# Work for the next attention layer, placed beside the last expert tiles of a two-layer decoder: sums in halves and later, first differences on another engine, row maxima behind the tiles

## The chip, the cores and the metric

One Trainium2 chip, one core of it. The metric is the device time of one execution in microseconds (us), the median of three runs. The core has a tensor engine (PE), a vector engine (VectorE, DVE in the rows), a scalar engine (ScalarE, ACT), GpSimd (POOL) and SyncE (SP), which here only issues DMAs. Each engine runs its own instructions in their written order, and the engines wait for each other through semaphores.

## The reference

Two decoder layers on x of shape (4, 512, 128) in float32: four batches of 512 tokens. Each layer is attention, cross-attention to a context of 77 keys, and a feed-forward part, each on a layer norm of x and added to x. The feed-forward part of layer 0 is a mixture of eight experts with the best two per token. What lies around the change:

```python
x = x + _L0_attn_ref(_layernorm(x, axis=-1), ...)        # causal, 16 heads of 8
x = x + _L0_xattn_ref(_layernorm(x, axis=-1), ctx_1024, ctx_1024, ...)
x = x + _L0_ffn_ref(_layernorm(x, axis=-1), ...)         # 8 experts, top 2 of them per token
x = x + _L1_attn_ref(_layernorm(x, axis=-1), ...)        # not causal, 16 heads of 8
x = x + _L1_xattn_ref(_layernorm(x, axis=-1), ctx_1024, ctx_1024, mask_1xSxS2_ff0, ...)
x = x + _L1_ffn_ref(_layernorm(x, axis=-1), ...)
```

## The kernel before

The core runs a first stream (attention and cross-attention of layer 0, 32 units of four heads and one batch each), then the experts (`moe_pe`, `moe_act`, `moe_dve`, `moe_pool`, `moe_sp`), then a second stream (attention of layer 1, here A1, 16 units, and the last layers).

**The expert tiles.** The tokens were scattered into rows sorted by expert. `BUSY_TILES` is 39: tiles t = 0 to 38 of 128 rows each. Every engine has a loop over t, in which its parts of neighbouring tiles stand in a fixed order:

- SP: the row number is read into a register (L1966), a wait for `y_at` of tile t-2 (L1969), the load of tile t into `x_in` (L1970), then `ahead_sp(e, t)`.
- PE: first half of the hidden layer of t+1 (L1897), turn of tile t+2 (L1888, a transpose, which waits for that tile's load), second half of the hidden layer of t+1, output of t (L1905), then `ahead_pe(e, t)`.
- ScalarE: SiLU of t (L1945), half of the weights of t+2 (L1935), `ahead_act(e, t)`.
- VectorE: `turned` of t+2 (L1753, L1754), `product` of t+1 (L1762), half of the weights of t+3 (L1767), `output` of t (L1774), `ahead_dve(e, t)`.
- GpSimd: the scatter of the finished tile t to HBM (L1874), which waits for VectorE's output of t, then `ahead_pool(e, t)`.

So in one round t the engines are not at the same tile: SP's load of t+4 follows VectorE's `turned(t+2)` of round t.

**The `ahead` functions** put work of the second stream between the rounds, each piece at a round t that is written out by hand. For batches 0 and 1 of x: from tile 22 on (`HALF_TILES` is 23) the outputs for these two batches are complete. `fetch_sp` brings them back from HBM (L1978, two DMAs of 512 KB). `combine_dve` adds the two weighted expert outputs to x (L1816, eight instructions of 128x128, four for each of the two experts). Then come the moments (L469 to L475), their root on GpSimd (L496), the norm (L490), its transpose on PE (L547), the copy (L561), and the q, k and v products (L864, L882).

**The three parts.** q and k are split into three bf16 parts that add up to the float32 value. `stage1_act` writes the first part (L1331) and a float32 copy `qf` (L1333, named `cos_sin` in the rows). GpSimd makes the first difference `rest = qf - part1` (L1344), ScalarE rounds it to the second part (L1337), and GpSimd makes the third (L1347). When the third is there, `stack_dma` writes the parts to HBM (L954, three DMAs of 384, 256 and 128 KB for q or for k), and `load_sp` loads them back in the layout of the heads (L663, L669, into `stk`). After that the row maxima of the scores can be made: `max_pe` (L598) and `max_dve` (L614), 16 of each for one unit of A1, then `neg_of` on GpSimd (L629, L631) and its transpose `turn_pe` (L636), with which the unit's scores can begin.

**PSUM banks.** `take_bank` hands out banks in turn; beside the tiles only two are free (`bank_scores[:, 3]` and `bank_pv`), behind them four.

Of the kernel before, what the change touches and what calls it, by code (L numbers as in the profile page):

```python
# [245 lines left out]

def qf_read_by(a, b, z):

    if a is X0 or b == 0:
        return split_number(a, b, 0 if a is A1 else z)  # L250
    return split_number(a, b - 1, z) + 1
# [11 lines left out]
def build(nc, d, out):  # L263
# [4 lines left out]
    with es:  # L268
# [650 lines left out]
        def split_pool(e, a, b, z, step):  # L919
# [10 lines left out]
            elif step == 2:  # L930
                e.wait_ge(s["rest"], n + 1)
# [395 lines left out]
        def stage1_act(e, b, z):  # L1327
# [4 lines left out]
            e.wait_ge(s["rest"], qf_read_by(A1, b, z))  # L1332
            e.activation(qf[:, z], bank_of(key), ACT.Identity, bias=bias).then_inc(is_emptied(key), 1)  # L1333

        def part2_act(e, b, z):
            e.wait_ge(s["rest"], split_number(A1, b, z) + 1)
            e.copy(parts[:, z, 1], rest[:, z]).then_inc(s["part2"], 1)  # L1337

        def split1_pool(e, b, z, step):
            n = split_number(A1, b, z)  # L1340
            if step == 0:
                e.wait_ge(s["part1"], n + 1)
                e.wait_ge(*emptied(("qk"[z], A1.ln, b)))
                e.tensor_tensor(rest[:, z], qf[:, z], parts[:, z, 0], ALU.subtract).then_inc(s["rest"], 1)  # L1344
            else:
                e.wait_ge(s["part2"], n + 1)
                e.tensor_tensor(parts[:, z, 2], rest[:, z], parts[:, z, 1], ALU.subtract).then_inc(s["part3"], 1)  # L1347
# [6 lines left out]
        def ahead_pe(e, t):  # L1354
            if t in (27, 33):
                norm_pe(e, A1.ln, t // 33)
            elif t == 28:
# [3 lines left out]
            elif t in (29, 36):  # L1361
                for part in range(2):
                    stage_v_pe(e, A1, t // 36, part)
            elif t in (34, 35):
                for part in range(2):
                    stage_q_pe(e, A1, 1, t - 34, part)
            elif t in (37, 38):
                for k in range(FIRST * (t - 37), FIRST * (t - 36)):
                    max_pe(e, A1.first, k)

        def ahead_act(e, t):
            if t in (29, 35):
                norm_act(e, A1.ln, t // 35)
            elif t in (30, 31):
                stage1_act(e, 0, t - 30)
            elif t == 32:
                part2_act(e, 0, 0)
                stage_v_act(e, A1, 0)
            elif t == 33:
                part2_act(e, 0, 1)  # L1380
            elif t in (36, 37):
                stage1_act(e, 1, t - 36)
            elif t == 38:
                part2_act(e, 1, 0)
                stage_v_act(e, A1, 1)
                part2_act(e, 1, 1)

        def ahead_dve(e, t):
            if t == 24:
                e.wait_ge(m["gates"], 1)  # L1390
            if t in (24, 28):
                combine_dve(e, 2, t // 28)
            elif t in (25, 30):
                moments_dve(e, A1.ln, t // 30)
            elif t in (26, 32):
                normalise(e, A1.ln, t // 32)
            elif t in (37, 38):
                for k in range(FIRST * (t - 37), FIRST * (t - 36)):
                    max_dve(e, A1.first, k)

        def ahead_pool(e, t):
            if t == 25:
                norm_pool(e, A1.ln, 0)
            elif t in (29, 35):
                split1_pool(e, t // 35, 0, 0)
            elif t in (30, 36):
                split1_pool(e, t // 36, 1, 0)
                if t == 30:
                    norm_pool(e, A1.ln, 1)
            elif t in (31, 37):  # L1410
# [1121 lines left out]
```

## Time and profile before

| | us |
|---|---|
| median of three runs | 761.88 (761.59, 761.88, 763.45) |
| the profiled execution | 766.63 |
| its span | 764.9 |
| PE busy | 645.7 (84%) |
| VectorE busy | 563.5 (74%) |
| ScalarE busy | 431.0 (56%) |
| GpSimd busy | 305.0 (40%) |
| tile 0 to 38, VectorE's outputs start | 346.2 to 474.2 |

The profiled execution took 4.75 us more than the median, and 1.7 us of it lie outside its span. The rows are of that one execution. "Full" clock of PE is 2.4 GHz (1.00 in the rows), half is 1.2 GHz (0.50). L12 is line 12 of the kernel as printed above. The L1774 instruction is run once per tile, 39 times; the 25th (tile 24) starts at 413.20, the 33rd (tile 32) at 450.56, the 35th (tile 34) at 457.13 and the last (tile 38) at 474.18.

### The profile page before, as it was taken

The numbers are of one execution on the slowest core, as the hardware profiler recorded it, in microseconds if no ns is written. First come the engines' busy times: TensorE is split into PE (matmuls) and PEld (weight loads), VectorE is DVE, ScalarE is ACT, GpSimd is POOL, SyncE is SP. The second block draws the span as 40 slices with busy tenths as digits, with TensorE's granted clock in tenths as the row PEclk, the third lists the DMA queues.
The fourth block names the chain that finished last, engine by engine and source line by source line (L and its number), as shares of the span: only waits on it lengthen the run. The fifth ranks groups of instructions, "written<-read, shape, count | busy, mean of one in ns | idle before, by whom it ended". The sixth has DMA issues, their size and how long they took to land.

```text
span 764.9 us, 16027 instructions
## 1 busy us (share of the span) xinstructions
PE 645.7 (84%) x5015; PEld 354.0 (46%) x5020; DVE 563.5 (74%) x1664; ACT 431.0 (56%) x825; POOL 305.0 (40%) x536
## 2 busy tenths in 40 slices
PE   5679998999978887239997987899999989897987
PEld 2344454444434444239997885133323323234543
DVE  6977688687737786747776686899998898924564
ACT  1415565566665654025664454478887777884644
POOL 6653454545551335723332354275251341421310
PEclk9867998999988999559999898599999999999998
DMA  7744564453233311211113126210413110000000
GB/s 229 253 162 146 174 197 142 127 179 99 75 87 85 110 45 67 78 36 47 50 47 92 35 72 213 98 57 30 139 51 116 30 55 30 2 1 1 15 15 28
DMA packets 72802, 67.17 MB, mean 88 GB/s; under 512 B 14560, under 2 KB 67232, under 8 KB 72720
## 3 DMA queue, kind: packets, MB, share of 16 engines
q1 hardware_dynamic: 69920, 61.21, 25.9%
q0 software_dynamic: 2272, 4.69, 1.9%
q8 instruction: 42, 0.69, 0.4%
q14 instruction: 40, 0.33, 0.1%
q10 hardware_dynamic: 528, 0.26, 0.1%
HBM read 37.74 MB, written 28.00 MB: 86 GB/s over the span
## 4 chain that ended last, share of the span: by engine, by line
PE 54%; DVE 23%; issue 9%; POOL 5%; ACT 4%; DMA 3%; SPq 1%; DVEq 0%; ACTq 0%; POOLq 0%
DVE mx L614 13%; PE bank_pv L761 11%; PE bank_turn L598 7%; PE bank_scores L2165 5%; PE bank_scores L713 4%; PE bank_scores L1897 4%; PE bank_turn L1897 4%; PE bank_scores L1905 4%; PE bank_turn L780 3%; POOL routed_tokens L1858 3%; DVE stats L469 2%; PE bank_turn L602 1%; DVE xn L490 1%; PE bank_turn L822 1%; ACT probs L734 1%
## 5 line engine op out<-in xcount | busy, mean ns | idle before, releaser
L614 DVE TENSOR_REDUCE mx<-bank_turn 128x1 f32<-128x512 f32 (+4 forms) x438 | 251.3, 612 | 45.7 <-PE bank_turn L602 29.6
L713 PE MATMUL bank_scores<-stk 64*128 64x512 bf16 (+3 forms) x576 | 172.6, 363 | 4.2 <-ACT probs L734 3.0
L598 PE MATMUL bank_turn<-stk 64*128 64x77 bf16 (+4 forms) x694 | 151.3, 305 | 27.8 <-DVE mx L614 18.7
L738 ACT ACTIVATE probs<-bank_scores 128x1024 f32<-128x1024 f32 (+4 forms) x160 | 116.8, 768 | 94.8 <-PE bank_scores L713 93.7
L734 ACT ACTIVATE probs<-bank_scores 128x512 f32<-128x512 f32 x256 | 139.1, 605 | 33.9 <-PE bank_scores L713 33.1
L761 PE MATMUL bank_pv<-probs,vsl 128*32 128x512 f32 (+3 forms) x1152 | 139.3, 556 | 2.9 <-POOL probs L746 1.8
L598 PEld LDWEIGHTS bank_turn<-stk 64*128 64x128 bf16 x694 | 52.0, 98 | 123.9 <-DVE mx L614 58.0
L746 POOL TENSOR_SCALAR_AFFINE_SELECT probs<-probs 128x256 f32<-128x256 f32 x128 | 51.6, 407 | 75.2 <-ACT probs L738 73.5
L1874 POOL DMA_INDIRECT expert_outputs<-probs,y_at x39 | 37.9, 972 | 95.4 <-DVE y_at L1754 61.3
L713 PEld LDWEIGHTS bank_scores<-stk 64*128 64x128 bf16 x576 | 45.8, 94 | 27.5 <-ACT probs L734 15.4
L496 POOL TENSOR_TENSOR rstd<-var,mhalf 128x4 f32<-128x4 f32 x24 | 24.7, 1028 | 78.3 <-DVE var L475 77.9
L614 DVE TENSOR_REDUCE mx<-bank_scores 128x1 f32<-128x512 f32 x73 | 49.7, 680 | 8.0 <-PE bank_scores L598 7.7
L602 PE MATMUL bank_turn<-masked_key,later_key 64*128 64x64 bf16 x512 | 51.3, 201 | 0.0
L602 PEld LDWEIGHTS bank_turn<-masked_key,later_key 64*128 64x128 bf16 x512 | 46.0, 103 | 11.3 <-issue 3.1
L2165 PE MATMUL bank_scores<-f_w1c,w 128*128 128x512 f32 x96 | 46.1, 618 | 0.4 <-ACT w L556 0.4
L1897 PE MATMUL bank_scores<-probs,w_now 128*128 128x128 f32 x304 | 41.9, 287 | 5.4 <-DVE probs L1753 5.4
L1905 PE MATMUL bank_scores<-w,oT 128*128 x312 | 42.9, 282 | 1.6 <-DVE probs L1774 1.6
L1897 PE MATMUL bank_turn<-probs,w_now 128*128 128x128 f32 x320 | 42.9, 284 | 0.0
L1897 PEld LDWEIGHTS bank_scores<-probs,w_now 128*128 128x128 f32 x304 | 39.5, 203 | 5.8 <-DVE probs L1753 5.7
L1897 PEld LDWEIGHTS bank_turn<-probs,w_now 128*128 128x128 f32 x320 | 40.9, 201 | 0.1
L1905 PEld LDWEIGHTS bank_scores<-w,oT 128*128 128x128 f32 x312 | 39.1, 197 | 2.3 <-issue 2.3
L761 PEld LDWEIGHTS bank_pv<-probs,vsl 128*32 128x32 f32 x1152 | 23.2, 109 | 33.3 <-issue 25.7
(310 smaller groups left out, 1062.6 us busy)
## 6 DMA issues: line engine op xcount, KB each, us to landing
stk<-stack_A SPq DMA_DIRECT2D x64, 256.0 KB, 3.1
w<-in_M_w SPq DMA_DIRECT2D x12, 512.0 KB, 4.4
stack_A<-parts SPq DMA_DIRECT2D x12, 384.0 KB, 2.7
stack_A<-fill SPq DMA_DIRECT2D x8, 512.0 KB, 5.0
stk<-stack_X SPq DMA_DIRECT2D x16, 256.0 KB, 2.7
stack_A<-parts SPq DMA_DIRECT2D x12, 256.0 KB, 3.1
probs<-routed_tokens SPq DMA_DIRECT2D x39, 65.0 KB, 1.9
stack_A<-parts SPq DMA_DIRECT2D x12, 128.0 KB, 2.9
```

The source lines that it names most:

```text
L598: mm = e.matmul(o, stk[r, slot, 0, pp, qt * P:(qt + 1) * P], stk[r, slot, 1, pp, 0:keys], start=True, stop=not a.causal)
L602: mm = e.matmul(o[:, qt * P + HR * k:qt * P + HR * (k + 1)], later_keys(j, k), masked_keys(j), start=False, stop=k == 1)
L614: e.tensor_reduce(o.rearrange("p h q -> p q h"), bank_of((g, m))[:, 0:k * keys].rearrange("p (q h k) -> p q h k", q=len(tiles), h=len(hs)) ...
L713: mm = e.matmul(score_bank(g, kt, i)[:, 0:S - q0], stk[r, slot, 1, pp, kt * P:(kt + 1) * P], stk[r, slot, 0, pp, q0:S], start=True, stop=True)
L734: e.activation(probs[:, probs_of(g, kt), j + 2 * pp], score_bank(g, kt, i), ACT.Exp, scale=1 / math.sqrt(HD)).then_inc(s["probs"], 1)
L738: e.activation(probs[0:a.kp, probs_of(g, kt), j:HG:2, 0:n], bank_scores[0:a.kp, 2 * j:2 * j + 2, 0:n], ACT.Exp, scale=1 / math.sqrt(HD)).t ...
L746: e.affine_select(out=o, in_=o, compare_op=ALU.is_ge, fill=0.0, base=0, pattern=[[0, 2], [1, P]], channel_multiplier=-1).then_inc(s["maske ...
L761: mm = e.matmul(bank_pv[VW * h:VW * (h + 1), q0:S], vsl[:, slot, kt, h, :], probs[:, probs_of(g, kt), h, 0:S - q0], start=(kt == 0), stop= ...
L1874: e.indirect_dma_start(scr_y, bass.IndirectOffsetOnAxis(ap=y_at[:, t:t + 1], axis=0), y_sb[:, t % 2], None).then_inc(m["stored"][t % 2], 16)
L1897: mm = e.matmul(hid[t % 2][z][:, c * P:(c + 1) * P], w_now[:, t % 2, o:o + P], x_inT[:, t % 2], start=True, stop=True)
L1905: mm = e.matmul(y_bank[:, 0:D], act[:, t % 2, c * P:(c + 1) * P], w2[:, bass.ds(ex[t], 1), c, :].rearrange("p o n -> p (o n)"), start=(c = ...
L2165: e.matmul(bank, f_xT[:, b, j * P + tap:j * P + tap + P], f_w1c[:, tap], start=(tap == 0), stop=False)
```

## The change

Only the work beside tiles 24 to 38 and what follows it directly is touched. `combine_dve` does four instructions at a time: batch 0 at rounds 25 and 26 instead of all eight at 24, batch 1 at 29 and 30 instead of 28. Moments move from 25 and 30 to 27 and 31, norms from 26 and 32 to 28 and 32, PE's transposes from 27 and 33 to 29 and 34, q and k of batch 0 from 28 to 31, and so on. The float32 copy `qf` and GpSimd's first difference are gone: VectorE computes it from the PSUM bank in one instruction (`rest1_dve`, bias added, first part subtracted). No maxima are made beside the tiles; all 16 of unit 32 follow them. Of batch 1, v's copy, the second parts and the third parts are made behind the tiles, its stacks after the shift of the first unit.

```diff
+        def rest1_dve(e, b, z):
+            key, n, bias = ("qk"[z], A1.ln, b), split_number(A1, b, z), wts["A1"]["bk" if z else "bq"][:]
+            e.wait_ge(s["part1"], n + 1)
+            e.wait_ge(s["part3"], n - 1 if b else 3 * NB + 1)
+            e.scalar_tensor_tensor(rest[:, z], bank_of(key), bias, parts[:, z, 0], ALU.add, ALU.subtract)\
+                .then_inc(is_emptied(key), 1)
...
-        def split1_pool(e, b, z, step):
...
+        def part3_1_pool(e, b, z):
+            e.wait_ge(s["part2"], split_number(A1, b, z) + 1)
+            e.tensor_tensor(parts[:, z, 2], rest[:, z], parts[:, z, 1], ALU.subtract).then_inc(s["part3"], 1)
...
         def ahead_dve(e, t):
-            if t == 24:
+            if t == 25:
                 e.wait_ge(m["gates"], 1)
-            if t in (24, 28):
-                combine_dve(e, 2, t // 28)
+            if t in (25, 26):
+                combine_dve(e, 0, t - 25)
+            elif t in (29, 30):
+                combine_dve(e, 1, t - 29)
...
+            elif t in (32, 33):
+                rest1_dve(e, 0, t - 32)
+                if t == 32:
+                    normalise(e, A1.ln, 1)
+            elif t in (37, 38):
+                rest1_dve(e, 1, t - 37)
...
         def ahead_pool(e, t):
...
+                part3_1_pool(e, 0, t - 34)
...
         def ahead_sp(e, t):
             if t == 27:
                 fetch_sp(e, 0)
-            elif t == 37:
-                stack_dma(e, A1, 0, 0)
+            elif t in (36, 37):
+                stack_dma(e, A1, 0, t - 36)
             elif t == BUSY_TILES - 1:
-                stack_dma(e, A1, 0, 1)
                 for g in range(A1.first, A1.first + UNITS):
                     load_sp(e, g)
+                fetch_sp(e, 1)
+                shift_sp(e, A1.first)
                 for z in range(2):
                     stack_dma(e, A1, 1, z)
-                shift_sp(e, A1.first)
-                fetch_sp(e, 1)
...
         def second_stream_pe(e):
...
-            for k in range(2 * FIRST, len(A1.items)):
-                max_pe(e, A1.first, k)
+            all_maxima_pe(e, A1.first)
...
         def second_stream_act(e):
+            stage_v_act(e, A1, 1)
+            for z in range(2):
+                part2_act(e, 1, z)
```

What this does to three queues is seen in the order of their instructions (line numbers are of the kernel whose order it is). On SP, before, from the load of tile 36 over that of tile 37 (both into `probs`), q's stack of batch 0 and the load of tile 38 to k's stack:

```order
L1966 TENSOR_LOAD tile_row
L1966 ISA x2
L1970 ISA [waits M0_y_at,M0_xT]
L1970 DMA probs<-routed_tokens 128x130
L954 DMA stack_A<-parts 128x3x512 [waits att_part3]
L954 DMA stack_A<-parts 128x2x512
L954 DMA stack_A<-parts 128x512
L1966 TENSOR_LOAD tile_row
L1966 ISA x2
L1970 ISA [waits M0_y_at,M0_xT]
L1970 DMA probs<-routed_tokens 128x130
L954 DMA stack_A<-parts 128x1536 [waits att_part3]
```

On SP now, from the load of tile 36 over q's stack, the load of tile 37 and k's stack to the row number of tile 38:

```order
L1966 DMA probs<-routed_tokens 128x130
L959 DMA stack_A<-parts 128x3x512 [waits att_part3]
L959 DMA stack_A<-parts 128x2x512
L959 DMA stack_A<-parts 128x512
L1962 TENSOR_LOAD tile_row
L1962 ISA x2
L1966 ISA [waits M0_y_at,M0_xT]
L1966 DMA probs<-routed_tokens 128x130
L959 DMA stack_A<-parts 128x1536 [waits att_part3]
L959 DMA stack_A<-parts 128x1024
L959 DMA stack_A<-parts 128x512
L1962 TENSOR_LOAD tile_row
```

The stacks moved up: before, q's stack stood behind the load of tile 37 and k's behind that of tile 38, the last; now they stand behind the loads of 36 and 37. On GpSimd, before, behind the scatter of tile 29 (scatters are `expert_outputs`, the first differences L1344 and the third parts L1347 of batch 0 stand between them):

```order
L1344 TENSOR_TENSOR rest<-cos_sin,parts 128x512 [waits emptied4,att_part1]
L1874 DMA expert_outputs<-probs,y_at 4116x128 [waits M0_y_out,M0_y_at]
L1344 TENSOR_TENSOR rest<-cos_sin,parts 128x512 [waits emptied3,att_part1]
L496 TENSOR_TENSOR rstd<-var,mhalf 128x4 [waits s_var]
L1874 DMA expert_outputs<-probs,y_at 4116x128 [waits M0_y_out,M0_y_at]
L1347 TENSOR_TENSOR parts<-rest,parts 128x512 [waits att_part2]
L1874 DMA expert_outputs<-probs,y_at 4116x128 [waits M0_y_out,M0_y_at]
L1347 TENSOR_TENSOR parts<-rest,parts 128x512 [waits att_part2]
```

On GpSimd now, the same kinds of instruction, from the scatters of tiles 32 to 34 to that of tile 36:

```order
L1870 DMA expert_outputs<-probs,y_at 4116x128 [waits M0_y_out,M0_y_at] x3
L1351 TENSOR_TENSOR parts<-rest,parts 128x512 [waits att_part2]
L1870 DMA expert_outputs<-probs,y_at 4116x128 [waits M0_y_out,M0_y_at]
L1351 TENSOR_TENSOR parts<-rest,parts 128x512 [waits att_part2]
L1870 DMA expert_outputs<-probs,y_at 4116x128 [waits M0_y_out,M0_y_at]
```

Batch 0's third parts followed the scatters of tiles 31 and 32; now they follow those of 34 and 35, and the first differences are no longer here. On VectorE, before, from the output of tile 24 (L1774) over batch 0's sums (L1816) to the turned tile 27 (L1753):

```order
L1774 TENSOR_TENSOR probs<-bank_scores,b_rows 128x128
L1816 SCALAR_TENSOR_TENSOR x_sb<-got,gate,x_sb 128x128 [waits M0_got0,M0_gates]
L1816 SCALAR_TENSOR_TENSOR x_sb<-got,gate,x_sb 128x128 x3
L1816 SCALAR_TENSOR_TENSOR x_sb<-got,gate,x_sb 128x128 [waits M0_weighed] x4
L1753 COPY probs<-bank_turn 128x128 [waits M0_weighed,M0_xT]
```

On VectorE now, one tile later, from the output of tile 25 (L1770) over the first half of the sums (L1811) to the turned tile 28 (L1749):

```order
L1770 TENSOR_TENSOR probs<-bank_scores,b_rows 128x128
L1811 SCALAR_TENSOR_TENSOR x_sb<-got,gate,x_sb 128x128 [waits M0_got0,M0_gates]
L1811 SCALAR_TENSOR_TENSOR x_sb<-got,gate,x_sb 128x128 x3
L1749 COPY probs<-bank_turn 128x128 [waits M0_xT]
L1750 SCALAR_TENSOR_TENSOR y_at<-probs,tile_f 128x1
```

Four of the eight sums are left there; the other four follow the output of tile 26.

## Rows read from the trace of the kernel before

**Rows 1.** Busy time by stretch: engines, granted clock, DMA share, GB/s.
```profile
345.00:390.00 45.00, 45.00 (x406) 45.00 (x405) 33.56 (x130) 26.69 (x82) 14.91 (x16) 1.00 0.18 48
...
414.00:419.00 5.00, 1.35 (x13) 1.16 (x11) 2.19 (x8) 1.25 (x4) 0.96 (x1) 0.95 0.48 166
419.00:422.00 3.00, 2.62 (x12) 2.62 (x13) 2.92 (x16) 0.39 (x2) 0.22 (x1) 0.50 0.09 22
...
474.00:484.00 10.00, 5.89 (x16) 1.14 (x16) 7.88 (x14) 0.00 (x0) 3.08 (x5) 0.50 0.29 106
```
**Rows 2.** Timeline of VectorE, tiles 23 to 26: start, duration, line, idle before.
```profile
410.40 0.28 DVE L1774 TENSOR_TENSOR probs<-bank_scores,b_rows 128x128 f32<-128x128 f32 x1
...
411.82 1.13 DVE L1762 SCALAR_TENSOR_TENSOR oT<-bank_scores,b_cols,probs 128x128 f32<-128x128 f32 x4 [0.58 <-ACT probs L1945]
...
413.20 0.28 DVE L1774 TENSOR_TENSOR probs<-bank_scores,b_rows 128x128 f32<-128x128 f32 x1
416.70 2.19 DVE L1816 SCALAR_TENSOR_TENSOR x_sb<-got,gate,x_sb 128x128 f32<-128x128 f32 x8 [3.23 <-DMA got<-expert_outputs]
...
422.27 0.17 DVE L475 TENSOR_SCALAR var<-mv 128x4 f32<-128x4 f32 x1
```
**Rows 3.** The chain that ended last, in order of time: start, duration.
```profile
405.20 0.89 PE bank_scores L1897 x8
...
410.92 5.68 DMA got<-expert_outputs
...
419.38 2.08 PE bank_scores L1897 x8
421.67 1.71 PE bank_scores L1897 x8
```
**Rows 4.** SP's issues, two stretches: start, duration of issuing.
```profile
410.92 0.94 SPq L1978 DMA_DIRECT2D got<-expert_outputs  x2
412.67 0.36 SPq L1970 DMA_DIRECT2D probs<-routed_tokens  x1
...
454.39 1.69 SPq L954 DMA_DIRECT2D stack_A<-parts  x3
457.84 0.36 SPq L1970 DMA_DIRECT2D probs<-routed_tokens  x1
```
**Rows 5.** DMA issues with time to landing: the load at 412.67.
```profile
probs<-routed_tokens SPq DMA_DIRECT2D x1, 65.0 KB, 5.7
```
**Rows 6.** The same view: the load at 457.84.
```profile
probs<-routed_tokens SPq DMA_DIRECT2D x1, 65.0 KB, 1.9
```
**Rows 7.** VectorE's timeline: moments beside GpSimd, outputs of tiles 32, 34.
```profile
443.73 1.73 DVE L475 TENSOR_SCALAR var<-mv 128x4 f32<-128x4 f32 x1
...
450.56 0.28 DVE L1774 TENSOR_TENSOR probs<-bank_scores,b_rows 128x128 f32<-128x128 f32 x1
...
457.13 0.29 DVE L1774 TENSOR_TENSOR probs<-bank_scores,b_rows 128x128 f32<-128x128 f32 x1
```
**Rows 8.** GpSimd's timeline: first difference, scatter of tile 32, third part.
```profile
444.26 1.16 POOL L1344 TENSOR_TENSOR rest<-cos_sin,parts 128x512 f32<-128x512 f32 x1
...
451.59 0.98 POOL L1874 DMA_INDIRECT expert_outputs<-probs,y_at  x1 [1.25 <-DVE probs L1774]
452.61 1.16 POOL L1347 TENSOR_TENSOR parts<-rest,parts 128x512 bf16<-128x512 f32 x1
```
**Rows 9.** One line of VectorE: min/median/max ns.
```profile
L1293 DVE SCALAR_TENSOR_TENSOR probs<-bank_scores,A_bq,cos_sin x4: 735/738/750, 13.8 to 41.0; 128x512 f32<-128x512 f32 x4
```
**Rows 10.** PE's timeline: turn of unit 32.
```profile
483.54 0.29 PE L636 MATMUL bank_turn<-identb,neg 128*32 128x128 bf16 x1 [2.40 <-POOL neg L631]
```
**Rows 11.** VectorE's timeline: output of tile 38, maxima of unit 32.
```profile
474.18 0.29 DVE L1774 TENSOR_TENSOR probs<-bank_scores,b_rows 128x128 f32<-128x128 f32 x1 [0.97 <-PE bank_scores L1905]
...
478.00 1.88 DVE L614 TENSOR_REDUCE mx<-bank_turn 128x1 f32<-128x512 f32 x3
...
482.19 0.68 DVE L614 TENSOR_REDUCE mx<-bank_scores 128x1 f32<-128x512 f32 x1
```

More of the change, by code:

```diff
@@ L1360, in ahead_pe @@
                         stage_q_pe(e, A1, 0, z, part)
-            elif t in (29, 36):
+            elif t in (33, 38):
                 for part in range(2):
-                    stage_v_pe(e, A1, t // 36, part)
-            elif t in (34, 35):
[L1365 to L1368, printed above, removed]
-                    max_pe(e, A1.first, k)
[L1371 to L1386, printed above, removed]
@@ L1388, in ahead_dve @@
-        def ahead_dve(e, t):
-            if t == 24:
-                e.wait_ge(m["gates"], 1)
-            if t in (24, 28):
-                combine_dve(e, 2, t // 28)
[L1393 to L1410, printed above, removed]
-                split1_pool(e, t // 37, 0, 1)
-            elif t in (32, 38):
-                split1_pool(e, t // 38, 1, 1)
-            elif t == 34:
+                    stage_v_pe(e, A1, t // 38, part)
+            elif t in (36, 37):
+                for part in range(2):
+                    stage_q_pe(e, A1, 1, t - 36, part)
@@ new lines, in ahead_act, with ahead_dve @@
+        def ahead_act(e, t):
+            if t in (31, 36):
+                norm_act(e, A1.ln, t // 36)
+            elif t in (32, 33):
+                stage1_act(e, 0, t - 32)
+            elif t == 34:
+                part2_act(e, 0, 0)
+            elif t == 35:
+                part2_act(e, 0, 1)
+                stage_v_act(e, A1, 0)
+            elif t in (37, 38):
+                stage1_act(e, 1, t - 37)
+        def ahead_dve(e, t):
+            if t == 25:
+                e.wait_ge(m["gates"], 1)
+            if t in (25, 26):
+                combine_dve(e, 0, t - 25)
+            elif t in (29, 30):
+                combine_dve(e, 1, t - 29)
+            elif t in (27, 31):
+                moments_dve(e, A1.ln, t // 31)
+            elif t == 28:
+                normalise(e, A1.ln, 0)
+            elif t in (32, 33):
+                rest1_dve(e, 0, t - 32)
+                if t == 32:
+                    normalise(e, A1.ln, 1)
+            elif t in (37, 38):
+                rest1_dve(e, 1, t - 37)
@@ L1415, in ahead_pool @@
+        def ahead_pool(e, t):
+            if t in (27, 31):
+                norm_pool(e, A1.ln, t // 31)
+            elif t in (34, 35):
+                part3_1_pool(e, 0, t - 34)
+            elif t == 36:
                 values_pool(e, A1.first)
@@ L1559, in second_stream_dve @@
         def second_stream_dve(e):
-            for k in range(2 * FIRST, len(A1.items)):
-                max_dve(e, A1.first, k)
+            all_maxima_dve(e, A1.first)
             turn_dve(e, A1.first)
@@ L1577, in second_stream_pool @@
             neg_of(e, A1.first)
+            for z in range(2):
+                part3_1_pool(e, 1, z)
             bias_pool(e, A1, 0)
```

50 lines of the change are left out of this document (21 added, 29 removed).

## The prediction

> **What bounds the kernel now.** I read the busy times by stretch first, then the chain that ended last, then the timelines of VectorE, PE, GpSimd and SP between tiles 24 and 38, and the times from issue to landing.
>
> In the tiles, PE is the bound: busy 45.00 of 45 us at full clock [rows 1]. A tile takes 2.79 us, from one output of VectorE to the next (410.40 to 413.20), and VectorE waits 0.58 us for ScalarE in it [rows 2]. PE's three groups of eight take 0.89 each at full clock and 1.71 at half, the turn 0.11 and 0.21 (2.79 less three times 0.89, and twice that) [rows 3].
>
> At tile 24 that ends. VectorE, with the output of tile 24 issued at 413.20, waits 3.23 us for batch 0's expert outputs, which were fetched at 410.92 and took 5.68 us, and then needs 2.19 us for eight sums [rows 2, 3]. PE gets nothing from it: 1.35 us busy of 5. When PE starts again at 419.38 its clock is 0.50, and the next group takes 2.08 us instead of 0.89 [rows 1, 3]. From tile 24 to tile 34 VectorE's outputs go from 413.20 to 457.13, 43.9 us for ten tiles that would take 27.9 [rows 2, 7]; to tile 38 it is 474.18, the last maximum of unit 32 starts at 482.19 and its turn at 483.54 [rows 10, 11]. Everything behind that turn is the same program in both kernels, so I take the shift of the turn for the shift of the end.
>
> **Part 1, tiles 24 to 34: a gain of 7.8 us.** The load of tile 28 was issued at 412.67, behind the two fetches of 512 KB, and landed after 5.7 us, at 418.4 [rows 4, 5]. That was hidden by VectorE's wait. It is next in line now: PE's turn of tile 28 is due 2.7 us ahead of the output of tile 26, at 416.1, and waits until 418.4. This is 2.3 us; VectorE's half sum (1.1 us, half of 2.19 [rows 2]), which can start at 416.7, lies inside it. I take full clock after it, since PE idles 2.3 us and not 4.
>
> From there to the output of tile 34: ten tiles of 2.79 (27.9), the 2.3 us, and PE's own additions: the transpose of a norm (0.44, half a group of eight), q and k (two times 0.9: an estimate, four instructions of 256 columns against a group of eight of 128 at 0.89 [rows 3]), v (0.89): 3.1 us. VectorE's additions in rounds 26 to 33 are three half sums (3.3), two rounds of moments (1.5 each: four statistics, four aggregates and L475, which ends at 422.44 [rows 2]), two norms (1.1 each, four instructions of the size of a half sum's four) and two of the new first differences. The nearest row for these is the same kind of instruction on the same size from PSUM, 0.74 us [rows 9]; 0.68, a maximum of that size [rows 11], is the lower end, and nothing makes more than 1.2 likely, what GpSimd took for it [rows 8]. Sum 10.0 us. Against it stand 0.6 us of free time in each of nine tiles, 5.4, and PE's 3.1, in which VectorE is free too: 8.5. The surplus is 1.5; placed tile by tile in the orders of both engines it comes to 2.8, since the additions of rounds 31 to 33 (1.5, 1.8, 0.7) come last and free time of earlier tiles cannot be kept for them. So the output of tile 34 starts at 413.2 + 27.9 + 2.3 + 3.1 + 2.8 = 449.3, where it was 457.13 [rows 7].
>
> In this I have left out that GpSimd blocks VectorE. L475, 0.17 us alone [rows 2], took 1.73 and ended with GpSimd's first difference [rows 7, 8], and before tile 34 there were three such hits. Six of the eight long GpSimd instructions leave the tiles, so the price in this stretch is nothing. The Trainium skill, page SBUF — State Buffer, section SBUF: two separate sides, says that GpSimd and an instruction of VectorE with two SBUF inputs or in a two-port mode lock each other out. By that rule the new difference, with one input in PSUM, is not blocked; if it were, as L475 was, the two would cost 1.6 us each and the output would start at 452.5.
>
> **Part 2, tiles 35 to 38: a loss of 14.3 us.** This is the term that decides. On SP, q's stack of batch 0 now stands ahead of the load of tile 37, and waits for q's third part. On GpSimd this third part stands behind the scatter of tile 34, which waits for VectorE's output of tile 34. So the load of tile 37 cannot be issued before the output of tile 34, although PE needs that tile for its turn in round 35, before the output of tile 35. From the output of tile 34: the scatter starts 1.03 later (450.56 to 451.59 [rows 7, 8]) and ends 0.98 later, the third part takes 1.16 more: 3.2 us. Three DMA issues 1.69, and the load is issued 3.45 after the first of them (454.39 to 457.84 [rows 4]), because the row number is read behind them. It lands 1.9 later [rows 6]. That makes 3.2 + 3.45 + 1.9 = 8.6 us; the turn is due about 1.3 us after the output of tile 34. PE is idle for 7.3 us, falls to half clock as in rows 3 after 4 us, and needs 0.21 + 1.71 + 1.71 to the output of tile 35, with 0.1 to VectorE: 12.3 us for this tile.
>
> The same chain holds once more: k's third part behind the scatter of tile 35, k's stack ahead of the load of tile 38. Another 12.3 us. The outputs of tiles 35 and 36 start at 461.6 and 473.9. Then come PE's q of batch 1 at half clock (1.9), the hidden layer of tile 38 in two groups (1.1 while the clock rises, 0.9), output 37 (0.9), k (0.9) and output 38 (0.9), with 0.1: 480.6. Before, tile 34 to tile 38 took 17.05 us (457.13 to 474.18), and included four serial maxima; now 31.3.
>
> **Part 3, behind the tiles: a loss of 2.3 us.** PE makes v (0.9), then the 16 maxima. They have four banks and go at VectorE's pace, 0.60 each (seven from 478.00 to 482.19 [rows 11]): the first starts 1.4 us after output 38, the last starts 9.0 later, at 491.0. From the last maximum to the turn it is 1.35 (482.19 to 483.54 [rows 10, 11]): 492.3. The first heads' loads are not in the way: k's stack is issued by 467, 15 us ahead of the first maximum. Batch 1's third parts (two of 1.16) follow the first unit's `neg_of`, and its stacks the shift; the first loads that need them stand in unit 33, a whole unit behind the turn. The earlier second fetch is issued about 485 and is done when the shift comes. I take zero for all three.
>
> Sum: 492.3 - 483.5 = +8.8 us, that is -7.8 + 14.3 + 2.3. Against the profiled execution this is 766.63 + 8.8 = 775.4; the median of the runs lies 4.75 below that execution, so 761.88 + 8.8 = 770.7.
>
> **Bounds.** Below: behind the fetch the load's issue came 0.8 us after the last issue ended (411.86 to 412.67 [rows 4]) and not 1.76, which gives back 1.9 in two stalls; if the clock stayed full after them, 3.7 more; if the maxima and the first scores of unit 32 ran at full clock where they ran at 0.50 [rows 1], up to 2. That is +1.2. Above: half clock after the 2.3 us at tile 28 (+2.5), the differences at 1.2 us or blocked (+1 to 3.2), half clock through tile 38 (+1.5): +13 to +15.
>
> **The rivals.**
> - *The tiles' gain stays and the stacks cost nothing* (faster). If load 37 did not have to stand behind the stack, tiles 35 to 38 would take 4 x 2.79 and PE's additions of 2.2: output 38 at 462.7, the turn 11.7 later at 474.4, and some 2 us more if the loads of `stk` hold the maxima (an estimate: they then follow k's stack with as little room as before): -7.1, or 754.8. For it: the order of the stretch before 34 is better in every term. Against it: SP's queue is in order, and the load is behind the waiting DMA. It decides from the point where each of the two stalls costs under 3.5 us; I count 9.
> - *The clock is worse than I take it* (slower still): the wait at tile 28 drops it, and so it does not recover between the two stalls and tile 38: +13, or 775. For it: half clock stood from 474 to 484 with PE busy 5.89 of 10 [rows 1].
> - *The stalls are cheaper*: row number early, the clock full in the maxima: +3.5, or 765.4. For it is the 0.8 us above.
> - *The change does nothing here*: the two parts cancel within 0.3%, for example one stall only. I see no way to it but chance.
>
> **How the numbers follow.** Forecast 0.66, worse clock 0.13, cheaper stalls 0.12, the gain without stalls 0.06, cancelled 0.03. A measurement of this kernel tells 0.3% (2.3 us) from no change. Slower: 0.66 + 0.13 + 0.12 = 0.91; same 0.03; faster 0.06. The time is 770.7. The range goes from the cheaper stalls to the worse clock, 764.8 to 775.8; the forecast's own is 767.5 to 774.
>
> **What would show it.** PE should wait twice for `probs<-routed_tokens` at L1884, some 7 us each, with the clock at 0.50 behind each, and SP's waits for GpSimd's third part should be the longest of that stretch. The load of tile 28 should hold PE for about 2 us near 416, and the wait for `got` shrink to under 1. The output of tile 34 should start near 449, that of tile 38 near 481, the turn of unit 32 near 492. If the outputs of tiles 35 and 36 follow at under 5 us, the prediction is wrong in part 2; if that of tile 34 comes later than 453, in part 1.

## The result: slower, by 4 to 9 us

| | before | after |
|---|---|---|
| median, first comparison | 761.74 (757.96 to 763.45, 4 runs) | 770.53 (764.69, 769.42, 771.64, 774.39) |
| ratio, with its 95% interval | | 1.0102 [1.0052, 1.0153] |
| median, second comparison | 763.42 (35 runs) | 768.13 (12 runs) |
| ratio, with its 95% interval | | 1.0058 [1.0027, 1.0090] |
| profiled execution, its span | 766.63, 764.9 | 769.42, 767.2 |
| output 24 to output 34 | 43.93 | 34.45 |
| output 34 to output 38 | 17.05 | 30.06 |
| output 38 to turn of unit 32 | 9.36 | 11.62 |
| these three together | 70.34 | 76.13 |

The slowdown was forecast as 8.8 us. The executions of one kernel lie up to 10 us apart, so a median of four says little about 3 us. The first ratio gives +4.0 to +11.7 us with its interval. The second comparison gives +4.4 us (0.58% of 763.4; by its interval 2.1 to 6.9 us). The one profile of each between output 24 and the turn gives +5.8 us. Start to output 24, the same program in both, took 3.3 us less in the profile of after (output 24 at 409.91, not 413.20), and from the turn to the end it is 281.2 us, where it was 281.4. (A second profile of after has 284.7 us there, so one pair of profiles says nothing below 3.5 us about that last part.) So I compare the stretches between the same instructions, and take the medians as a check.

The page of the kernel after (busy time, share, instructions; then the clock in 40 slices). The columns of the second fence are those of [rows 1].

```profile
PE 641.1 (84%) x5015; PEld 351.5 (46%) x5020; DVE 558.6 (73%) x1668; ACT 428.8 (56%) x821; POOL 300.7 (39%) x532
...
PEclk9967998999989999569999978599999999999998
```
```profile
345.00:390.00 45.00, 45.00 (x406) 45.00 (x405) 33.56 (x130) 26.36 (x81) 15.32 (x16) 1.00 0.19 51
412.00:415.00 3.00, 0.96 (x9) 0.77 (x7) 0.78 (x3) 1.65 (x5) 0.00 (x0) 1.00 0.40 130
444.50:452.40 7.90, 0.55 (x5) 0.36 (x4) 0.14 (x1) 2.26 (x7) 2.12 (x2) 0.73 0.36 116
452.40:454.40 2.00, 1.97 (x9) 1.97 (x10) 0.42 (x2) 0.00 (x0) 0.00 (x0) 0.50 0.00 0
457.00:464.00 7.00, 1.03 (x5) 0.74 (x4) 0.00 (x0) 1.14 (x4) 2.15 (x2) 0.74 0.37 132
```

Tiles 0 to 23 are as in [rows 1], PE-bound. The busy totals fell on every engine. What grew is idle time of PE, 0.55 busy in 7.9 us and 1.03 in 7. PE's timeline shows why (in brackets the idle time ahead and what ended it):

```profile
415.04 0.33 PE L1884 MATMUL bank_turn<-ident,probs 128*128 128x128 f32 x1 [2.08 <-DMA probs<-routed_tokens]
...
452.44 0.48 PE L1884 MATMUL bank_turn<-ident,probs 128*128 128x128 f32 x1 [7.39 <-DMA probs<-routed_tokens]
...
454.41 1.91 PE L1901 MATMUL bank_scores<-w,oT 128*128 x8
...
464.47 0.47 PE L1884 MATMUL bank_turn<-ident,probs 128*128 128x128 f32 x1 [6.43 <-DMA probs<-routed_tokens]
...
486.04 0.29 PE L641 MATMUL bank_turn<-identb,neg 128*32 128x128 bf16 x1 [2.52 <-POOL neg L636]
```

Two waits for a tile's load, 7.4 and 6.4 us, each with the half clock behind it (granted clock 0.50 from 452.4 to 454.4 and again from 464.4 to 468.5); the last row answers to [rows 10]. SP's timeline shows what the loads stood behind:

```profile
447.56 1.58 SPq L959 DMA_DIRECT2D stack_A<-parts  x3
...
450.58 0.35 SPq L1966 DMA_DIRECT2D probs<-routed_tokens  x1
...
459.72 1.31 SPq L959 DMA_DIRECT2D stack_A<-parts  x3
...
462.51 0.35 SPq L1966 DMA_DIRECT2D probs<-routed_tokens  x1
```

and SP's waits between 413 and 500 name their cause (sum, count, longest), with GpSimd's timeline behind it:

```profile
SPq L959 <- POOL parts L1351: 19.9, 2, 11.1
```
```profile
445.39 0.96 POOL L1870 DMA_INDIRECT expert_outputs<-probs,y_at  x1 [1.94 <-DVE probs L1770]
446.38 1.16 POOL L1351 TENSOR_TENSOR parts<-rest,parts 128x512 bf16<-128x512 f32 x1
```

Read upwards: the load of tile 37 is issued at 450.58, behind q's stack (447.56), which waits for GpSimd's third part (446.38 to 447.54), which stands behind the scatter of tile 34 (445.39), which waits for VectorE's output of tile 34. That output, on VectorE's timeline, is at 444.36:

```profile
415.02 0.29 DVE L1770 TENSOR_TENSOR probs<-bank_scores,b_rows 128x128 f32<-128x128 f32 x1 [2.24 <-DMA expert_outputs<-probs,y_at]
415.22 1.13 DVE L1811 SCALAR_TENSOR_TENSOR x_sb<-got,gate,x_sb 128x128 f32<-128x128 f32 x4
...
422.95 0.17 DVE L480 TENSOR_SCALAR var<-mv 128x4 f32<-128x4 f32 x1
...
438.08 0.74 DVE L1342 SCALAR_TENSOR_TENSOR rest<-bank_pv,A_bq,parts 128x512 f32<-128x512 f32 x1
...
444.36 0.28 DVE L1770 TENSOR_TENSOR probs<-bank_scores,b_rows 128x128 f32<-128x128 f32 x1
...
456.47 0.29 DVE L1770 TENSOR_TENSOR probs<-bank_scores,b_rows 128x128 f32<-128x128 f32 x1 [0.25 <-PE bank_scores L1901]
...
468.50 0.29 DVE L1770 TENSOR_TENSOR probs<-bank_scores,b_rows 128x128 f32<-128x128 f32 x1 [0.58 <-PE bank_scores L1901]
...
474.42 0.29 DVE L1770 TENSOR_TENSOR probs<-bank_scores,b_rows 128x128 f32<-128x128 f32 x1 [1.12 <-PE bank_scores L1901]
```

Outputs 34, 35, 36 and 38: tiles 35 and 36 take 12.1 and 12.0 us, where 34 to 38 took 17.05 in all. The sums that waited 3.23 us for `got` in [rows 2] wait no more; L480 and the first difference take 0.17 and 0.74, where L475 took 1.73 in [rows 7].

### The profile page after: what moved, and what is told of

It reads as the page before. It is cut to its first block, busy times and chain, and to the rows that moved or that the text cites. A ratio compares the mean times of both kernels' runs of the same rounds, so it can differ in the third digit from the quotient of the medians.

```text
span 767.2 us, 16024 instructions
## 1 busy us (share of the span) xinstructions
PE 641.1 (84%) x5015; PEld 351.5 (46%) x5020; DVE 558.6 (73%) x1668; ACT 428.8 (56%) x821; POOL 300.7 (39%) x532
## 4 chain that ended last, share of the span: by engine, by line
PE 55%; DVE 23%; issue 9%; POOL 6%; ACT 4%; DMA 3%; SPq 1%; DVEq 0%; ACTq 0%; POOLq 0%
DVE mx L619 13%; PE bank_pv L766 11%; PE bank_turn L603 7%; PE bank_scores L2161 5%; PE bank_turn L1893 5%; PE bank_scores L1901 4%; PE bank_scores L718 4%; PE bank_scores L1893 4%; POOL routed_tokens L1854 2%; PE bank_turn L785 2%; DVE stats L474 2%; DMA probs<-routed_tokens 2%; PE bank_turn L607 2%; DVE xn L495 1%; PE bank_turn L827 1%
## 5 line engine op out<-in xcount | busy, mean ns | idle before, releaser
L619 DVE TENSOR_REDUCE mx<-bank_turn 128x1 f32<-128x512 f32 (+4 forms) x444 | 254.6, 612 | 45.0 <-PE bank_turn L607 28.7
L603 PE MATMUL bank_turn<-stk 64*128 64x77 bf16 (+4 forms) x700 | 152.9, 302 | 29.8 <-DVE mx L619 19.4
L718 PE MATMUL bank_scores<-stk 64*128 64x512 bf16 (+3 forms) x576 | 170.5, 358 | 4.2 <-ACT probs L739 3.0
L619 DVE TENSOR_REDUCE mx<-bank_scores 128x1 f32<-128x512 f32 x68 | 46.1, 678 | 5.0 <-PE bank_scores L603 5.0
L1941 ACT ACTIVATE probs<-bank_scores,b_cols 128x128 f32<-128x128 f32 x76 | 21.7, 369 | 31.5 <-PE bank_scores L1893 31.5
```

The costliest lines, as they stand in the source:

```text
L603: mm = e.matmul(o, stk[r, slot, 0, pp, qt * P:(qt + 1) * P], stk[r, slot, 1, pp, 0:keys], start=True, stop=not a.causal)
L619: e.tensor_reduce(o.rearrange("p h q -> p q h"), bank_of((g, m))[:, 0:k * keys].rearrange("p (q h k) -> p q h k", q=len(tiles), h=len(hs)) ...
L718: mm = e.matmul(score_bank(g, kt, i)[:, 0:S - q0], stk[r, slot, 1, pp, kt * P:(kt + 1) * P], stk[r, slot, 0, pp, q0:S], start=True, stop=True)
```

## The experiments

All are edits of the kernel after. In the table, us between the same instructions of one profile each (O24, O34 and O38 are the starts of VectorE's outputs of tiles 24, 34 and 38, "turn" is the start of the turn of unit 32); "median" and "ratio" are over all runs against the kernel before on the same chip (763.42 for the first four, 762.93 for the next four, 761.28 for the last three).

| kernel | O24-O34 | O34-O38 | O38-turn | O24-turn | median | ratio [95%] |
|---|---|---|---|---|---|---|
| before | 43.93 | 17.05 | 9.36 | 70.34 | | |
| after_again | 34.65 | 29.84 | 11.63 | 76.12 | 768.13 | 1.0058 [1.0027, 1.0090] |
| stacks_behind_38 | 34.52 | 12.96 | 12.78 | 60.26 | 757.03 | 0.9906 [0.9871, 0.9941] |
| stacks_37_and_38 | 34.27 | 19.66 | 11.33 | 65.26 | 758.27 | 0.9941 [0.9910, 0.9971] |
| q_stack_at_36 | 34.52 | 21.99 | 14.47 | 70.98 | 762.79 | 0.9989 [0.9959, 1.0020] |
| sums_from_24 | 35.24 | 12.90 | 13.01 | 61.15 | 755.30 | 0.9883 [0.9851, 0.9915] |
| sums_whole | 35.69 | 12.91 | 13.23 | 61.83 | 752.14 | 0.9872 [0.9841, 0.9904] |
| difference_on_pool | 34.99 | 12.17 | 16.28 | 63.44 | 755.86 | 0.9892 [0.9847, 0.9937] |
| parts3_at_33 | 34.91 | 11.20 | 11.80 | 57.91 | 752.40 | 0.9852 [0.9825, 0.9879] |
| parts3_at_33_again | 34.39 | 11.19 | 11.62 | 57.20 | 753.63 | 0.9885 [0.9837, 0.9932] |
| fetch_at_28 | 32.80 | 11.17 | 11.76 | 55.73 | 748.72 | 0.9838 [0.9794, 0.9882] |
| sums_whole_at_24 | 37.18 | 13.05 | 12.81 | 63.04 | 754.56 | 0.9924 [0.9887, 0.9962] |

The medians differ less than the stretches where stalls are taken out or put in. Against after, stacks_behind_38 is 15.9 us less from O24 to the turn and 11.1 us less by the medians; against stacks_behind_38, q_stack_at_36 is 10.7 us more by the stretch and 5.8 by the medians, stacks_37_and_38 5.0 and 1.2. Part of this is that each stretch is one execution: from the turn to the end, where the program is the same, these profiles have 281.2 to 284.7 us, and both ends of that range come from the two profiles of after. So the stretches show which wait came and went, and the medians what it was worth in the whole time.

### after_again: the same kernel once more

> The changed kernel once more, for its median and for how far its executions lie apart. My theory (two loads of tiles held on SP's queue) expects 767 to 772 us, and in the trace two waits of PE for a tile's load, 7.4 and 6.4 us, as in the first profile. If the first measurement owed its 8.8 us to chance in the stretches before the tiles, the ratio to the kernel before comes nearer to the 5.8 us that the two profiles show between the output of tile 24 and the turn of unit 32.

Its profile repeats the first within 0.3 us in each of the three stretches (not behind the turn, as said); its ratio is the smaller one of the result above.

### Where the stacks stand

stacks_behind_38:

```diff
-            elif t in (36, 37):
-                stack_dma(e, A1, 0, t - 36)
             elif t == BUSY_TILES - 1:
+                for z in range(2):
+                    stack_dma(e, A1, 0, z)
```

> Both stacks of batch 0 are issued behind the load of tile 38, all else as in the changed kernel. Theory (SP's queue holds the loads of tiles 37 and 38): both long waits of PE for a load go, tiles 34 to 38 take about 13.5 us and not 30.1, the maxima then start about 1 us later behind output 38 because k's stack and the loads of the heads come late; in all 15 us less than the changed kernel, about 755 us, and 6 to 8 us less than the kernel before. Rival 1 (the transfers themselves, 768 KB of parts and the loads behind them, are what costs): the wait moves to the loads of the heads, the maxima start 6 us or more late, and the whole is 765 or more. Rival 2 (VectorE's fuller rounds hold PE back): tiles 34 to 38 stay above 20 us.

Both waits are gone, O24 to turn falls by 15.9 us against after, and the kernel is faster than before. O34 to O38 takes 12.96 us (13.5 expected, over 20 by rival 2), and the maxima come 1.2 us later behind O38 (1 expected, 6 or more by rival 1). A smaller wait shows: ScalarE's first part of batch 1 overwrites what the stack reads (`ACT parts L1336 <- DMA stack_A<-parts`, longest 3.9 us), and PE waits for the loads of the heads, in its timeline:

```profile
460.86 0.59 PE L603 MATMUL bank_turn<-stk 64*128 64x512 bf16 x3 [1.10 <-DMA stk<-stack_A]
```

stacks_37_and_38 keeps the places that the kernel before had, `elif t == 37: stack_dma(e, A1, 0, 0)` and k's stack at the last tile:

> q's stack behind the load of tile 37, k's behind that of tile 38, as the kernel before had them; all else as in the changed kernel. Theory: no wait for the load of tile 37; the load of tile 38 lands 8.1 us after output 34 and is needed 4.5 us after it, so one wait of PE of 3 to 4 us, and with the clock at half behind it, if it falls, 2 to 3 us more: 4 to 7 us above the kernel with both stacks behind the load of tile 38. Rival (an engine's queue is not held by a DMA that waits): no wait, and the same time as that kernel.

```profile
452.27 0.48 PE L1885 MATMUL bank_turn<-ident,probs 128*128 128x128 f32 x1 [5.04 <-DMA probs<-routed_tokens]
```

One wait of 5.04 us where 3 to 4 were expected, and the tile takes 9.15. The stretch is 5.0 us longer than in stacks_behind_38, as expected (4 to 7), the median only 1.2. In before, with the stacks at these same places, PE waited for no tile's load between 455 and 484. So the old places are not harmless once the third parts come later: what counts is the distance from the third part to the stack, not the stack's round.

q_stack_at_36 (`elif t == 36` for q, k's stack at the last tile) keeps one stall of the two:

> Only q's stack stands ahead of the load of tile 37, k's is issued behind that of tile 38. Theory: exactly one wait of PE for a load, 7.4 us at tile 37, half clock for 5 to 6 us behind it, so 9 us above the kernel with both stacks behind and 6 to 7 us below the changed kernel: 762 to 765 us. Rival (the second stall of the changed kernel comes from the half clock or from the first stall, not from k's stack): no difference from the changed kernel in tile 38's load.

```profile
451.22 0.47 PE L1885 MATMUL bank_turn<-ident,probs 128*128 128x128 f32 x1 [8.24 <-DMA probs<-routed_tokens]
...
467.81 0.59 PE L603 MATMUL bank_turn<-stk 64*128 64x512 bf16 x3 [2.89 <-DMA stk<-stack_A]
```

One wait of 8.24 us (7.4 expected), and that tile takes 12.97. The load of tile 38 is not waited for, so the second stall of after is due to k's stack. Against stacks_behind_38 O34 to O38 is 9.0 us longer: this is the price of one stall in this stretch, and two of it (18.1) are about what after pays over stacks_behind_38 (17.1). By the medians one stall costs 5.8 us and the second 5.3. With one stall the kernel is level with before, 762.79 us, in the range expected.

### Where the sums stand

These three stand on stacks_behind_38, and part the gain of tiles 24 to 34. sums_from_24 makes the first half of batch 0's sums one round earlier:

```diff
-            if t == 25:
+            if t == 24:
                 e.wait_ge(m["gates"], 1)
-            if t in (25, 26):
-                combine_dve(e, 0, t - 25)
+            if t in (24, 26):
+                combine_dve(e, 0, t // 26)
```

> On the kernel with both stacks behind the load of tile 38: the first half of batch 0's sums goes back to round 24, the second half stays at 26. Theory (VectorE's wait for the fetch at round 24 costs what rows 1 to 3 show, and the load of tile 28 costs 2.2 us in any case behind it): VectorE waits 3.2 us again and PE idles about 3 us at one stretch instead of 2.2 at the load, the load of tile 28 then hides: 0.5 us more if the clock stays full, 3 to 3.5 more if it falls. From tile 24's output to the turn 60.8 or 63.6 us, where the kernel with both stacks behind has 60.3. Rival (the later round alone is the gain of part 1): 7 us more.

```profile
416.76 1.16 PE L1893 MATMUL bank_scores<-probs,w_now 128*128 128x128 f32 x8 [3.09 <-DVE probs L1749]
```

```profile
416.00:420.00 4.00, 3.24 (x27) 3.12 (x28) 3.66 (x16) 1.65 (x5) 0.84 (x1) 1.00 0.09 22
```

PE idles 3.09 us, the stretch behind it is at clock 1.00, and the load of tile 28 lies hidden in that idle time as in the kernel before. The later round is thus worth only 0.7 us of the stretch, as the theory had it: one wait is exchanged for another.

sums_whole puts the eight sums together at rounds 25 and 29 (`if t in (25, 29): for k in range(2): combine_dve(e, t // 29, k)`):

> On the kernel with both stacks behind the load of tile 38: all eight sums of a batch at once, at rounds 25 and 29, nothing of them at 26 and 30. Theory: VectorE has the same sum of work, 1.1 us more in one round and less in the next, and PE can be late by 1.3 us at most: 0.5 to 1.5 us more between the outputs of tiles 24 and 34 (34.5 there). Rival (halves matter, since a whole sum empties PE's lead): 2 us or more per batch and the clock falls, 4 us or more in all.

O24 to O34 is 1.2 us longer, as the theory had it (0.5 to 1.5) and not the rival's 4: halving the sums at these rounds is worth little. That the median is lower than its parent's (752.14) is within what executions differ by, and I give it no weight.

sums_whole_at_24 makes all eight of batch 0 at round 24, as before:

> On the kernel with both stacks behind the load of tile 38: all eight sums of batch 0 at round 24 as the kernel before had them, batch 1's in halves at 29 and 30. With the first half alone at 24 PE idled 3.1 us in one stretch and its clock stayed full; the kernel before had 4.0 us and fell. Theory (what the place at 24 cost was the fall of the clock more than the wait): PE idles 4.1 us, the clock falls, the tiles behind run at half for 5 to 6 us: 38 to 39.5 us between the outputs of tiles 24 and 34, where the first half alone has 35.2. Rival (the clock falls for another reason, such as what PE did earlier): 36.3 us, full clock.

```profile
411.56 1.16 PE L1893 MATMUL bank_scores<-probs,w_now 128*128 128x128 f32 x8 [4.09 <-DVE probs L1749]
412.72 1.92 PE L1893 MATMUL bank_scores<-probs,w_now 128*128 128x128 f32 x8
```
```profile
409.00:412.00 3.00, 0.44 (x4) 0.45 (x5) 2.85 (x12) 0.00 (x0) 0.00 (x0) 1.00 0.03 9
412.00:415.00 3.00, 3.00 (x19) 3.00 (x18) 1.74 (x8) 1.65 (x5) 0.95 (x1) 0.60 0.16 36
```

The idle stretch is the 4.1 us expected and the clock falls, where it had stayed full after 3.09 us. But it stood at 0.50 for only 3.3 us (412.7 to 416.0), not for the 5 to 6 expected and not for the 5.5 us of before (419.4 to 424.9) after the same idle time; I can't say why. So O24 to O34 is 37.18 and lies between the theory's 38 to 39.5 and the rival's 36.3. Against sums_from_24 it is 1.9 us. And 37.18 is still 6.75 less than before's 43.93: most of the gain does not lie at tile 24.

### The first differences on GpSimd again

difference_on_pool stands on stacks_behind_38; ScalarE writes the float32 copy again, and GpSimd takes the differences at rounds 32, 33, 37 and 38.

```diff
-            elif t in (32, 33):
-                rest1_dve(e, 0, t - 32)
-                if t == 32:
-                    normalise(e, A1.ln, 1)
-            elif t in (37, 38):
-                rest1_dve(e, 1, t - 37)
+            elif t == 32:
+                normalise(e, A1.ln, 1)
...
         def ahead_pool(e, t):
...
+            elif t in (32, 33):
+                rest1_pool(e, 0, t - 32)
...
+            elif t in (37, 38):
+                rest1_pool(e, 1, t - 37)
```

> On the kernel with both stacks behind the load of tile 38: the first differences of batches 0 and 1 on GpSimd as before, with the float32 copy on ScalarE, in the rounds 32, 33, 37 and 38. Theory (GpSimd's 1.16 us instructions block VectorE's instructions that stay in SBUF): one or two of the four strike L480, the weights' copy or y_at for 1.2 to 1.6 us; less 0.74 us of VectorE in rounds 32 and 33; the second part of batch 1 comes later: 1 to 3 us more from tile 24's output to the turn. Rival (GpSimd is free and VectorE the scarce engine): 0.5 to 1.5 us less.

VectorE's timeline, then GpSimd's:

```profile
433.88 1.89 DVE L1751 SCALAR_TENSOR_TENSOR y_at<-probs,tile_f 128x1 uint32<-128x1 f32 x1
...
438.63 1.95 DVE L1764 COPY w_now<-w 128x512 f32 x1
```
```profile
434.58 1.17 POOL L1344 TENSOR_TENSOR rest<-cos_sin,parts 128x512 f32<-128x512 f32 x1
...
439.11 1.17 POOL L1344 TENSOR_TENSOR rest<-cos_sin,parts 128x512 f32<-128x512 f32 x1
```

An instruction of VectorE on one column (0.21 us in after) takes 1.89 and ends with GpSimd's, at 435.77 and 435.75; the copy of weights, 0.42 in after, takes 1.95. The Trainium skill, page SBUF — State Buffer, section SBUF: two separate sides, states this lock for two SBUF inputs and for copies in a two-port mode; the trace agrees for both kinds. The page also says that whichever starts first has the ports; here VectorE's record starts first (433.88 against 434.58) and yet VectorE was held, so the starts in these records don't tell who had them. The cost to the stretch stayed small, though: two hits take 3.2 us of VectorE before O34, and O34 comes 0.5 later. O34 to O38 is even 0.8 shorter. The 3.5 us come behind tile 38, where PE waits 4.39 us for `stk` and its clock is at 0.50 afterwards. It starts the maxima 17.3 us after O34 instead of 14.8. SP issued the first loads of the heads at the same distance from O34 in both kernels (11.1 us), so they landed later and were not issued later; why is open. The whole stretch is 3.2 us longer, just above the 1 to 3 expected, but for the most part not by the holds that the theory named. By the whole times nothing is seen (ratios 0.9892 and 0.9906).

### The third parts one round earlier, and the fetch one round later

parts3_at_33 (on stacks_behind_38) has `elif t in (33, 34): part3_1_pool(e, 0, t - 33)`:

> On the kernel with both stacks behind the load of tile 38: batch 0's third parts one round earlier on GpSimd, at 33 and 34. There ScalarE waited 3.9 us for q's stack to be read out of the parts before it could write batch 1's first part, PE idled 1.9 us for that and 1.1 us for the loads of the heads. Theory: q's third part is done 2.8 us earlier, both waits go: 2.5 to 3 us less, about 57.5 us from tile 24's output to the turn and a median near 753 to 754. Rival: the second parts are not there yet at round 33, GpSimd waits and holds the scatter of tile 34: no gain.

ScalarE's wait and PE's for `stk` are gone: 2.35 us, just under the 2.5 to 3 expected. parts3_at_33_again is the same kernel beside the next one:

> The kernel with both stacks behind the load of tile 38 and third parts at rounds 33 and 34, once more, beside the next one and on the same chip: 57.9 us from tile 24's output to the turn of unit 32, ratio to the kernel before 0.983 to 0.988.

It repeats within 0.7 us (57.20; the ratio, 0.9885, lies just above the range expected). fetch_at_28 is that kernel with `if t == 28: fetch_sp(e, 0)` instead of 27, so that the fetch of 1 MB stands behind the load of tile 28:

> The same, and the first fetch is issued behind the load of tile 28 and not ahead of it. Theory (on one queue the load waits behind the fetches' bytes): PE's 2.1 us wait for the load of tile 28 goes. But VectorE's output of tile 25 waited 2.2 us for the scatter of tile 23 to land, which shares the DMA engines with the fetches, and the fetched outputs land 1 us later: so 0.5 to 1 us less in all, and VectorE's wait next in line, before output 25 or before the first half sum. Rival 1 (the load was the only thing): 2 us less. Rival 2 (the later landing of the fetch costs as much): 0 to 1 us more, and the wait of PE then begins at the load of tile 29.

```profile
416.47 0.29 DVE L1770 TENSOR_TENSOR probs<-bank_scores,b_rows 128x128 f32<-128x128 f32 x1 [0.17 <-DMA expert_outputs<-probs,y_at]
```
```profile
415.00:418.00 3.00, 3.00 (x30) 3.00 (x29) 2.83 (x12) 1.86 (x6) 0.91 (x2) 1.00 0.86 291
```

PE is busy through this stretch of the fetch (DMA share 0.86), and for 32.57 of the 32.80 us between O24 and O34; in parts3_at_33_again it waited 1.69 us for the load of tile 28. VectorE waits 0.17 instead of 1.66 there, and O24 to O34 is 1.6 us shorter (32.80 for 34.39). I had expected another wait in its place and 0.5 to 1 us in all; none came, as rival 1 had it, and the 1.5 us of the whole stretch lie between its 2 and my 1. The medians of these two differ by 4.9 us, more than the stretch explains. This version takes 748.72 us, 0.9838 [0.9794, 0.9882] of before on the same chip, the lowest ratio of the table.

## Why the prediction was right, point by point

**Part 2, the two stalls: right, shown by undoing them.** Forecast 31.3 us from output 34 to 38, measured 30.06. Forecast 8.6 us from output to landing, PE idle 7.3, 12.3 per tile; measured idle 7.39 and 6.43, tiles 12.11 and 12.03. The load was issued 6.2 us behind output 34 (444.36 to 450.58), where I had 6.65: the row number and its register cost 1.4 us behind the third issue and not 1.8. The forecast's 31.3 us are 1.2 us too long: 0.5 in the two stalled tiles and 0.8 in tiles 37 and 38. The cause was tested: without the stacks in front both waits go (stacks_behind_38), with one stack one wait stays (q_stack_at_36).

**Part 1, tiles 24 to 34: right in sign, 1.7 us too small.** Forecast 36.1 us for the ten tiles, measured 34.45. The mis-sized term is VectorE's surplus. With 27.9 for ten tiles, 2.1 for the load of tile 28 and 3.1 for PE's additions, 1.4 us are left for it. I had taken 2.8, placed tile by tile; the simple sum, 1.5, was the better one. (PE's 3.1 are right: its timeline has 0.44 for the transpose, 0.86 and 0.87 for q and k, 0.90 for v. And PE itself waits for VectorE nowhere in this stretch: it is busy 32.07 of 34.45 us, idle 2.08 for the load, and 0.27 for no wait that the profile shows. What VectorE adds makes its output start later behind PE's work, by about 1.1 us, 32.07 less 27.9 and 3.1, and does not stop PE.) Whether GpSimd would hold the new first difference no run shows, since no long instruction of GpSimd ran beside it.

Where the gain came from I had only partly. Stepwise, from the table: 6.75 us are there even with all sums of batch 0 at tile 24 (43.93 to 37.18), 1.9 come from halving them there (to 35.24), 0.7 from the later round (to 34.52). Most of the 6.75 lie in the tiles behind. PE is idle 8.52 us of this stretch in before and 4.09 in sums_whole_at_24, and busy 35.41 and 33.09. About 1.1 us of the difference in busy time is the half clock, which stood 2.2 us longer in before. The 4.0 us behind tile 24 are in both. What is idle beyond them in before are five waits, 4.5 us in all, of which before's PE timeline shows the three longest:

```profile
437.62 1.16 PE L882 MATMUL bank_pv<-A_wv,xnT 128*128 128x128 f32 x8 [1.12 <-ACT cos_sin L1333]
...
445.70 1.16 PE L1897 MATMUL bank_scores<-probs,w_now 128*128 128x128 f32 x8 [1.34 <-DVE probs L1753]
...
455.83 1.16 PE L1905 MATMUL bank_scores<-w,oT 128*128 x8 [1.05 <-DVE probs L1774]
```

The first is for ScalarE's float32 copy, which the change took out and which the bank of v's product had to wait for. The other two stand right behind instructions of VectorE that GpSimd held. In before, GpSimd's first difference held L475 (1.73 for 0.17) and its two third parts a `w_now` and a `y_at`, 4.1 us in all on VectorE; before's timelines of VectorE and of GpSimd, beside [rows 8]:

```profile
449.29 1.35 DVE L1767 COPY w_now<-w 128x512 f32 x1
...
451.99 1.81 DVE L1754 SCALAR_TENSOR_TENSOR y_at<-probs,tile_f 128x1 uint32<-128x1 f32 x1
```
```profile
449.17 1.17 POOL L1347 TENSOR_TENSOR parts<-rest,parts 128x512 bf16<-128x512 f32 x1
```

In after no instruction of VectorE in this stretch is held. But the first differences, put back on GpSimd, cost only 0.5 us up to output 34, and the third parts one round earlier 0.4 in one profile and nothing in the other, so in the new order such holds are mostly hidden, and they don't explain the 6.75 by themselves. What took before's five waits away, the missing copy, the missing holds, batch 1's halved sums or the moved moments, was not tried one by one and stays open.

**The load of tile 28: right.** PE waits 2.08 us for it (forecast 2.3), with the clock at 1.00 behind, as forecast. The load took 5.6 us [rows 5]. Not foreseen: VectorE waited 2.24 us in the same place for a scatter's landing, beside the same fetch, and not for `got`. By this reading it costs nothing on its own, since PE waits as well; a later fetch freed both at once (fetch_at_28).

**Part 3: right.** Forecast 11.7, measured 11.62, at VectorE's pace for 16 maxima. Behind the turn 281.2 against 281.4: nothing shows there of the three costs that I took at zero. But after_again has 284.7 for the same program, so costs of up to 3.5 us in that part are not excluded.

**The sum: size not settled below 4 us.** +8.8 was forecast and +8.8 came in the first medians, but that agreement is partly chance. The stretches say +5.8, the larger comparison +4.4, and by the forecast's own steps the missing 3 us are the 1.7 of part 1 and the 1.2 of part 2. The rival whose stalls cost nothing gave 754.8; the kernel in which they are gone takes 757.03. It was right on that kernel and wrong on this one, where each stall costs 9 us of the stretch (some 5.5 by the medians) and not under 3.5. One sum of the prediction is off: its upper bound, 8.8 + 2.5 + 1 to 3.2 + 1.5, is +13.8 to +16.0 and not +13 to +15.

## What to carry to other kernels

In these runs a DMA issue of SP that waited held every issue behind it, loads that depend on nothing of it too: before moving an issue, follow what it waits for back through the other engines, and ask whether a load behind it feeds an earlier piece of the same chain, as SP's load of tile 37 stood behind a result queued behind tile 34's scatter. Where a producer is moved later (the third parts here), its consumers must move as far, for even their old places can have become a stall. And where executions differ by 10 us, the time between two instructions close around the change, which both kernels have, tells a wait of 2 us that the medians of a few runs hide: for the two kernels measured twice, O24 to the turn repeated within 0.7 us. It doesn't tell what the change is worth to the whole: far behind it, the same program differed by 3.6 us between two profiles of one kernel.

## What the runs showed of the hardware

- The clock after idle time of PE within the tiles: 2.08 (after) and 3.09 us (sums_from_24) left it at 1.00; after 4.03 (before), 4.09 (sums_whole_at_24, one group later), 5.04 (stacks_37_and_38), 6.43 and 7.39 us (after) it was at 0.50, and a group of eight then took 1.7 to 2.1 us. Long idle stretches are not the only way down: beside the maxima of stacks_behind_38 the clock fell at about 463 (mean 1.00 from 459 to 463, 0.52 from 463 to 472), where PE's idle stretches just before were 1.86 and 1.10 us and PE was busy 2.07 of 4 us.
- A load of 65 KB right behind a fetch of 1 MB in its queue landed after 5.6 us and not 1.9, and GpSimd's scatters beside the same fetch landed after 4.4 to 6.6 us and not 2.3. With the fetch issued behind the load (fetch_at_28), PE waited for neither, and VectorE 0.17 us for a scatter.
- VectorE's instructions that GpSimd held began before GpSimd's in the records and ended with it or soon after: 433.88 to 435.77 beside 434.58 to 435.75, and 438.63 to 440.58 beside 439.11 to 440.28 (difference_on_pool).
